# Next-chunk query and key/value products placed among a tile's scores in the index stage of a seven-stage macaron block

## What is computed

```
qi = hadamard((x @ wq_idx).reshape(B, S, Hi, Di))
ki = hadamard(x @ wk_idx)
iw = x @ w_iw
logits = jax.nn.relu(jnp.einsum('bthd,bsd->bhts', qi, ki))
I = jnp.einsum('bth,bhts->bts', iw, logits)
I = jnp.where(causal, I, NEG)
vals, idx = jax.lax.top_k(I, TOPK)
```

## Time and profile before

| | us |
|---|---|
| median of three runs | 2803.31 |
| lowest and highest | 2797.86, 2806.11 |
| profiled execution | 2802.95 |
| its span | 2801.2 |
| index scores and searches, about 1468 to 2030 | 562 |

### The profile page before, as it was taken

The page is one execution under the profiler, slowest core; times in us unless marked ns, Lnnn a source line. Parts: engine busy times, 40 slices in busy tenths (PEclk is TensorE's granted clock), DMA queues, the critical chain, the costliest instruction groups (busy, mean ns, idle before and its releaser), DMA issues. The chain is left out here.

```text
span 2801.2 us, 44746 instructions
## 1 busy us (share of the span) xinstructions
PE 2432.0 (87%) x15815; PEld 1884.3 (67%) x15815; DVE 1718.2 (61%) x3579; ACT 1343.7 (48%) x2718; POOL 1086.9 (39%) x989
## 2 busy tenths in 40 slices
PE   4967899999998986969979898898879998888798
PEld 4855555555555545858867776777668877776687
DVE  7556765756847727554456988979825454545443
ACT  3434355455464453432239868767644443433222
POOL 2542112102112112632317645636356666757232
PEclk9987999999999986989989999999989999999999
DMA  5242000000000003240010000000033233323200
GB/s 164 80 125 73 9 24 9 19 17 19 9 9 19 2 26 120 87 146 31 1 46 1 1 8 1 1 8 9 1 134 89 84 95 89 101 82 100 83 1 30
DMA packets 77332, 136.58 MB, mean 49 GB/s; under 512 B 25792, under 2 KB 47256, under 8 KB 75968
## 3 DMA queue, kind: packets, MB, share of 16 engines
q0 software_dynamic: 26336, 73.01, 8.7%
q1 hardware_dynamic: 50784, 60.72, 6.7%
HBM read 112.48 MB, written 20.81 MB: 48 GB/s over the span
## 5 line engine op out<-in xcount | busy, mean ns | idle before, releaser
L1448 ACT ACTIVATE PT<-ps 128x512 f32<-128x512 f32 (+3 forms) x640 | 298.1, 536 | 336.0 <-PE ps L1205 335.7
L2310 POOL DMA_INDIRECT KV<-kv_scratch,sidx x384 | 368.0, 958 | 213.1 <-issue 131.8
L35 PE MATMUL ps<-KIh,qih 128*128 128x512 f32 (+2 forms) x640 | 247.4, 387 | 50.4 <-DVE Isc L1894 40.0
L1325 DVE TENSOR_REDUCE xn<-ps 128x1 f32<-128x512 f32 x384 | 240.9, 682 | 41.0 <-PE ps L1190 38.7
L1954 POOL TENSOR_TENSOR part_sum<-part_sum,rlp 128x1024 f32<-128x1024 f32 (+7 forms) x120 | 210.6, 1755 | 84.6 <-ACT rlp L1780 83.4
L1894 DVE SCALAR_TENSOR_TENSOR Isc<-ps,iw,Isc 128x1024 f32<-128x1024 f32 (+7 forms) x216 | 208.6, 966 | 50.3 <-ACT ps L1804 45.1
L36 PE MATMUL ps<-KIl,qih 128*128 128x512 f32 (+2 forms) x640 | 239.2, 374 | 0.0
L37 PE MATMUL ps<-KIh,qil 128*128 128x512 f32 (+2 forms) x640 | 238.6, 373 | 0.0
L2232 ACT ACTIVATE sP<-sP,snm 128x128 f32<-128x128 f32 (+2 forms) x256 | 110.4, 432 | 232.8 <-DVE snm L2295 226.7
L1804 ACT ACTIVATE ps<-ps,iwa 128x1024 f32<-128x1024 f32 (+7 forms) x240 | 198.2, 858 | 46.4 <-PE ps L37 45.9
L35 PEld LDWEIGHTS ps<-KIh,qih 128*128 128x128 f32 x640 | 124.2, 194 | 95.0 <-issue 74.0
(11 more groups left out here) (356 smaller groups left out, 6743.6 us busy)
## 6 DMA issues: line engine op xcount, KB each, us to landing
cs<-in_rope SPq DMA_DIRECT2D x20, 512.0 KB, 4.1
ycomb<-y_rows SPq DMA_DIRECT2D x16, 512.0 KB, 4.9
w1raw<-in_w SPq DMA_DIRECT2D x14, 512.0 KB, 6.7
KV<-kv_scratch,sidx POOLq DMA_INDIRECT x384
xn_rows<-xnr SPq DMA_DIRECT2D x8, 512.0 KB, 4.9
w2raw<-in_w SPq DMA_DIRECT2D x14, 256.0 KB, 7.1
wir<-in_wi SPq DMA_DIRECT2D x1, 2176.0 KB, 7.9
X<-in_x SPq DMA_DIRECT2D x1, 2048.0 KB, 8.1
```

The lines of the kernel that those rows point to most:

```text
L35: pe.matmul(out, lhs[0], rhs[0], start=start, stop=False)
L1325: v.tensor_reduce(part, o, AX_X, ALU.max).then_inc(a_free, 1)
L1448: s.activation(PT[:, rnd % 2, hh, lo:CH], ps[:, BANK[kind, u, j, r, hh % 2], lo:CH], ACT.Exp, scale=SCALE).then_inc(a_exp, 1)
L2310: g.indirect_dma_start(KV[:, BG * (k % RB) + m, :], None, a["kv_scratch"], bass.IndirectOffsetOnAxis(sidx[:, t % 2, at:at + 1], 0)).then_i ...
```

## The change

The last pass of tiles 12, 8 and 4 takes in the next chunk's items: behind each of its first four units stands a kv item, and behind each odd head the query pair of that head and the one before it. Only the first chunk is still prepared ahead of its scores. For tiles 12, 8 and 4 the order of the passes is reversed, so that the last one is the 1024-wide one (tile 4 has one pass of 640). The cast of a query pair waits for that pass's unit of the odd head instead of the tile's last unit. `signs` comes after the last subtraction of a chunk, not ahead of the first. The search steps are spread over the units and query pairs of the tile that they now stand in. Nothing is computed that was not before.

```diff
         def iunits(t):
-            return [(h, lo, min(WIDE, (t + 1) * P - lo)) for lo in range(0, (t + 1) * P, WIDE) for h in range(NHI)]
+            starts = list(range(0, (t + 1) * P, WIDE))
+            if t % CT == 0:
+                starts.reverse()
+            return [(h, lo, min(WIDE, (t + 1) * P - lo)) for lo in starts for h in range(NHI)]
+
+        def last_pass(t):
+            return iunits(t)[-1][1]
+
+        def prepared_for(c):
+
+            kv = [("kv", t, 0) for t in reversed(range(CT * c, CT * (c + 1)))]
+            return kv, [("q", NCH - 1 - c, pair) for pair in range(QP)]
+
+        def line(t):
+
+            out, units = [], [(t, h, lo) for h, lo, w in iunits(t)]
+            if t == TILES - 1:
+                kv, q = prepared_for(NCH - 1)
+                out += kv + q
+            if t % CT != 0 or t == 0:
+                return out + units
+            kv, q = prepared_for(t // CT - 1)
+            out += units[:-NHI]
+            for h, unit in enumerate(units[-NHI:]):
+                out.append(unit)
+                if h < CT:
+                    out.append(kv[h])
+                if h % 2 == 1:
+                    out.append(q[h // 2])
+            return out
...
         for t_ in TILE_ORDER:
...
+            for key_ in line(t_):
+                QUEUE[key_] = inumber
+                inumber += 1
+                if key_[0] == t_:
+                    SCORED[key_] = iscored
+                    PASSED[t_, key_[2]] = ipassed // NHI
+                    iscored, ipassed = iscored + 1, ipassed + 1
...
-            return POOLED * (PASSED[t, (passes(t) - 1) * WIDE] + 1)
+            return POOLED * (PASSED[t, last_pass(t)] + 1)
...
+            for key in ITEMS:
+                room(key)
+                o = ibanks(key)
+                if key[0] == "kv":
...
+                elif key[0] == "q":
...
+                else:
+                    t, h, lo = key
+                    d, w = NCH - 1 - t // CT, min(WIDE, (t + 1) * P - lo)
+                    tok = slice(t % CT * P, (t % CT + 1) * P)
+                    pe.wait_ge(i_ql, QP * d + h // 2 + 1)
...
                     s.wait_ge(i_q, QP * d + pair + 1)
-                    if d >= 1 and pair == 0:
-                        s.wait_ge(i_L, SCORED[CT * (c + 1), NHI - 1, (passes(CT * (c + 1)) - 1) * WIDE] + 1)
+                    if d >= 1:
+                        t = CT * (NCH - d)
+                        s.wait_ge(i_L, SCORED[t, 2 * pair + 1, last_pass(t)] + 1)
...
-                s.wait_ge(i_iw, 4 * (d + 1))
...
+                    s.wait_ge(i_iw, 4 * (NCH - t // CT))
+                    s.wait_ge(i_L, SCORED[key] + 1)
...
+            for t in TILE_ORDER:
+                p = TILES - 1 - t
+                todo = [key for key in line(t) if key[0] != "kv"]
+                first = [key for key in todo if key[0] == t][0]
+                steps_done = 0
+                for at, key in enumerate(todo):
+                    if key[0] == "q":
+                        d, pair = key[1:]
+                        v.wait_ge(i_qh, QP * d + pair + 1)
+                        v.tensor_tensor(qil[:, 2 * pair:2 * pair + 2, :].rearrange("p h t -> p (h t)"), ibanks(key),
+                                        qih[:, 2 * pair:2 * pair + 2, :].rearrange("p h t -> p (h t)").bitcast(F32),
+                                        ALU.subtract).then_inc(i_ql, 1)
+                        if pair == QP - 1:
                             signs(d)
...
+                    while p >= 1 and steps_done < (at + 1) * searches(t + 1) // len(todo):
+                        topk_step(t + 1, steps_done)
+                        steps_done += 1
```

More of the change, by code:

```diff
@@ L1712, in room @@
                         pe.wait_ge(i_A, added(*before))
[L1714 to L1719, removed]
+            for key in ITEMS:
+                room(key)
+                o = ibanks(key)
+                if key[0] == "kv":
+                    tok = slice(key[1] * P, (key[1] + 1) * P)
                     for k in range(KD):
-                        i = product(pe, ibanks(key)[:, 0:KVI], (XTh[:, k, tok], XTl[:, k, tok]),
+                        i = product(pe, o[:, 0:KVI], (XTh[:, k, tok], XTl[:, k, tok]),
                                     (ikv_h[:, k, :], ikv_l[:, k, :]), k == 0, k == KD - 1)
                     i.then_inc(i_kv, 1)
[L1724 to L1727, removed]
+                elif key[0] == "q":
+                    d, pair = key[1:]
                     for m in range(2):
@@ L1730, in index_tensor @@
                         for k in range(KD):
-                            i = product(pe, o[:, CH * m:CH * (m + 1)], (wih[:, h, k, :], wil[:, h, k, :]), xt(k, c), k == 0, k == KD - 1)
+                            i = product(pe, o[:, CH * m:CH * (m + 1)], (wih[:, h, k, :], wil[:, h, k, :]), xt(k, NCH - 1 - d),
+                                        k == 0, k == KD - 1)
                     i.then_inc(i_q, 1)
[L1733 to L1744, removed]
+                else:
[3 more added lines that the diff above has]
+                    pe.wait_ge(i_ql, QP * d + h // 2 + 1)
+                    for at in range(0, w, CH):
+                        wide = max(min(CH, w - at), 2 * P)
+                        i = product(pe, o[:, at:at + wide], (qih[:, h, tok], qil[:, h, tok]),
+                                    (KIh[:, lo + at:lo + at + wide], KIl[:, lo + at:lo + at + wide]), True, True)
+                    i.then_inc(i_L, 1)
             pe.wait_ge(i_k, SEARCHED[-1] + 1)
@@ L1780, in signed @@
                 s.activation(at, at, ACT.Copy, scale=iws[:, t, h:h + 1]).then_inc(i_sg, 1)
-            for d in range(NCH):
-                c = NCH - 1 - d
-                for t in reversed(range(CT * c, CT * (c + 1))):
+            for key in ITEMS:
+                if key[0] == "kv":
+                    t = key[1]
                     p = TILES - 1 - t
-                    o = ibanks(("kv", t, 0))
+                    o = ibanks(key)
                     s.wait_ge(i_kv, p + 1)
@@ L1791, in index_scalar @@
                     s.copy(kvs[:, p % 2, :], o[:, 0:2 * P]).then_inc(i_kve, 1)
-                for pair in range(QP):
+                elif key[0] == "q":
+                    d, pair = key[1:]
                     s.wait_ge(i_q, QP * d + pair + 1)
-                    if d >= 1 and pair == 0:
-                        s.wait_ge(i_L, SCORED[CT * (c + 1), NHI - 1, (passes(CT * (c + 1)) - 1) * WIDE] + 1)
-                    s.copy(qih[:, 2 * pair:2 * pair + 2, :].rearrange("p h t -> p (h t)"), ibanks(("q", d, pair))).then_inc(i_qh, 1)
@@ new lines, in index_scalar @@
+                    s.copy(qih[:, 2 * pair:2 * pair + 2, :].rearrange("p h t -> p (h t)"), ibanks(key)).then_inc(i_qh, 1)
+                else:
+                    t, h, lo = key
+                    w = min(WIDE, (t + 1) * P - lo)
+                    o = ibanks(key)[:, 0:w]
+                    s.wait_ge(i_iw, 4 * (NCH - t // CT))
+                    s.wait_ge(i_L, SCORED[key] + 1)
+                    if h in VH:
+                        s.activation(o, o, ACT.Relu, scale=iwa[:, t, h:h + 1]).then_inc(i_R, 1)
+                        if before:
+                            signed(*before)
+                        before = None
+                    else:
+                        if before:
+                            signed(*before)
+                        m = counted(t, h, lo)
+                        if m >= RL:
+                            s.wait_ge(i_B, summed(*PKEYS[m - RL]))
+                        s.activation(rlp[:, m % RL, 0:w], o, ACT.Relu, scale=iwa[:, t, h:h + 1]).then_inc(i_R, 1)
+                        before = (t, h, lo, w) if h in SH else None
@@ L1903, in scores @@
                     i.then_inc(i_A, 1)
[L1905 to L1912, removed]
-                            signs(d)
[L1914 to L1925, removed]
@@ new lines, in index_vector @@
+            for t in TILE_ORDER:
[5 more added lines that the diff above has]
+                    if key[0] == "q":
+                        d, pair = key[1:]
+                        v.wait_ge(i_qh, QP * d + pair + 1)
[3 more added lines that the diff above has]
+                        if pair == QP - 1:
+                            signs(d)
+                    else:
+                        h, lo = key[1:]
+                        if p >= 2 and key == first:
+                            v.wait_ge(i_k, SEARCHED[t + 1])
+                        scores(t, h, lo, min(WIDE, (t + 1) * P - lo))
+                    while p >= 1 and steps_done < (at + 1) * searches(t + 1) // len(todo):
+                        topk_step(t + 1, steps_done)
+                        steps_done += 1
```

## The result

| | before | after |
|---|---|---|
| median of seven runs each, us | 2803.31 | 2816.37 |
| lowest and highest | 2797.86, 2811.17 | 2813.73, 2823.95 |
| profiled execution, its span | 2802.95, 2801.2 | 2813.73, 2811.9 |
| first score product to the first of tile 0 | 546.30 | 556.46 |

The ratio on record is 1.0040, 95% interval 1.0026 to 1.0054; the medians are 13 us apart. The changed kernel is slower by a little more than the 0.3% that can be told from no change, and its median lies outside the range of 2795 to 2811. The forecast of 2804.4 is 12 us too low.

What follows compares the result with a forecast made beforehand. TensorE was taken to bound chunk preparation and the wide pass right after it, VectorE the later passes. The terms −10.0 + 2.95 + 7.1 + 1.5 gave +1.5 us on 2802.95, so 2804.4 us, range 2795 to 2811.

Steps and rivals of the forecast that it cites:

- step 3: Hosts (passes of tiles 12, 8, 4 taking in the next chunk's items) end earlier on TensorE: 10.0 us gained.
- step 4: Behind the hosts, signs at the last pair start ACT 1.8 us later; 7.05 of the 10.0 us is left.
- Step 6: At the start, chunk 0 in tile 15 has the later signs and no gain: 1.5 us lost.
- Step 5: Behind the hosts, search steps pushed out of the query stretch lengthen the windows: 7.1 us given back.
- Step 1: TensorE's work in a host: 47.23 us for tiles 12 and 8, 41.63 for tile 4.
- Step 2: Reversed passes of tiles 12 and 8 cost nothing: their narrow passes stay at 19.50 and 10.65 us.
- Not all will lie at one end together: On the sum of all bounds, 2796.0 to 2814.8 us: the terms won't all reach their good or bad ends.
- the ring stalls in the host: Rival: slots free too late in the hosts, 0.5 us in each of 24 groups, 2816 us; chance 0.14.
- TensorE decides to the end: Rival: tiles behind hosts are paced by TensorE and ACT, no steps given back, 2793 us; chance 0.16.
- the clock: Rival: a low-clock stretch falls inside a host, 3.4 us each, two 6.8, 2808 to 2811 us; chance 0.08.

Runs made afterwards that it cites:

- kernel 1: Changed kernel with the signs after the second query pair instead of the last: scores stretch 549.29 us, ratio to before 1.0023.
- kernel 10: The changed kernel run and profiled again, nothing altered: 2818.23 us, ratio to before 1.0054, scores stretch 556.60 us.
- kernel 5: Changed kernel with the kv items behind the first four query pairs and signs at the fifth pair: scores stretch 542.79 us, ratio to before 0.9987.
- kernel 11: Same code as kernel 5, run on the first kind of chip: 2802.56 us, ratio to before 0.9991, scores stretch 546.52 us.
- kernel 8: Kernel 1 with all four kv items ahead of the host's first unit: scores stretch 549.24 us, ratio to before 1.0004.
- kernel 4: Changed kernel without the reversed passes of tiles 12 and 8: scores stretch 556.60 us, ratio to before 1.0057.
- kernel 3: Kernel before with no search steps beside the query pairs of chunks 1 to 3: scores stretch 551.41 us, ratio to before 1.0022.
- kernel 9: Kernel before with kv items behind query pairs 0 to 3 and signs at the fifth pair: 2804.40 us, ratio 0.9998, scores stretch 544.07 us.
- kernel 2: Kernel before with only the signs moved after the last subtraction: scores stretch 551.86 us, ratio to before 1.0014.

## Why the prediction was wrong

The forecast's mechanism held: what TensorE gained in the hosts was given back behind them. Its sizes did not: the gain (step 3) was 3.8 us, not 10.0, and the signs (steps 4 and 6) cost 5.2 to 7.2, not 4.45. The three terms, read on TensorE from the first score product of the host tile to the next chunk's first, and behind that:

| step | forecast, us | measured | by what |
|---|---|---|---|
| 3, hosts end earlier | −10.0 | −3.8 | windows before and after |
| 4 and 6, signs | +2.95 and +1.5 | +7.2, of which 5.2 in the tiles where they act | kernel 1; kernel 10 |
| 5, search steps | +7.1 | +6.6 | kernel 1 against before |
| sum | +1.5 | +10.0 | +10.2 in the stretch |

The terms are differences of single profiles, good to a microsecond or two each; in kernel 10 the hosts end 2.3 us earlier in sum, with a low clock in tile 12's narrow pass.

**Step 1** was right. Kernels 5 and 11 show wide hosts of 47.32 to 47.43 us for the 47.23 worked out. A full-width score unit still takes 1.40 us for its six products, 0.2333 each. The Trainium skill (TensorE: Matmul & The Clock Gate, "Wait — 56ns, not 53.3ns?") gives 215.7 ns; these products don't reach that.

**Step 3** is the one that failed most. "The same slots are waited for in the new order; I keep these": the pauses were 8.6 us, not 4.34, and thus at the upper bound in sum (twice). The reason, as far as kernels 5 and 8 show it, is that the queue behind the slot had changed. Before, kv items and long pairs filled the ring while VectorE had nothing else to do; in the new order each second slot holds a score unit that is added by VectorE, and the items between are the shortest of all, 0.77 us. Kernels 5 and 8 tell this apart: the same items in another order give 2.0, the kv items moved ahead of the entry 7.3. In addition the narrow passes that now come first are longer, from last add to last add 20.1 and 12.0 us against 19.50 and 10.65. So of step 3's 10.0 some 4.3 went into pauses and 2 into those two passes. Step 2 had these at "well under a microsecond", and that was wrong for tile 8, though kernel 4 shows that the reversal as a whole costs nothing.

**Steps 4 and 6** were right in kind and too small by 2.7 us, or by 0.8 if only the four tiles are counted in which the signs act. The wait on ACT was taken as 1.8 us longer than before; the idle time of its first activation rose by 3.05, 2.5 and 2.1 in tiles 11, 7 and 3, and by 1.7 in tile 15. Part is the first sign operation, 1.49 us for 0.18 in tile 11 and 1.04 in tile 7. Part of the 7.2 is the clock: behind the pause of 2.43 us on TensorE it was 0.51 for 3.4 us in one profile, which cost 1.25, and 1.00 in the other, so the pause doesn't decide it by itself. Step 6 alone erred the other way: tile 15 took 45.45 us for 45.06, so the start cost 0.4 and not 1.5.

**Step 5** was right, +7.1 against +6.6 (5.3 in kernel 5, 5.1 in kernel 3). All eleven steps among the units leave VectorE no idle time to fill, as tile 6 had said.

"Not all will lie at one end together" was the wrong way to narrow the range. As I read it, the entry pauses and the signs have one cause in common, VectorE late with the operation that lets another engine go; the pauses came out at their upper bound, and the signs of step 4 had no bound at all. The bad end of the sum, 2814.8, is near the measured time partly by luck: it takes 12.8 us for the steps, which cost 4 to 7. Of the rivals, *the ring stalls in the host* named the right chain (subtraction, step, add) but priced it at 0.5 us in each of 24 groups; there is none in the steady groups (5.55 us each in tiles 12 and 8, 4.84 in tile 4), and 4.3 us more at the three entries. That its 2816 is the measured time is chance. *TensorE decides to the end* was wrong, *the clock* never fell inside a host (granted 1.00 in all three) and mattered behind one.

What stays open: the median differs by 13.1 us and the stage by 10.2. The 4.4 us behind the stage are not explained. They come again: from tile 0's first product to the end it is 787.2 and 786.6 us in the kernel before and kernel 9, and 791.5, 790.9 and 791.6 in the changed kernel, kernel 10 and kernel 11. Ahead of the stage the same three are shorter (1463.9, 1467.1 and 1464.1 against 1467.8 and 1469.7), and the two parts together are 2255 to 2258 in all five, so no loss outside the stage is shown.

## What to carry to other kernels

Moving work of the bounding engine in among other work of the same engine saves only what the other engine did beside it, so ask what that stretch had been hiding (here the search steps and the signs) before counting a gain. Where a ring of buffers is drained by an engine in arrears, give each slot that comes free the longest item: here that order took the pauses from 8.6 to 2.0 us, and with no interleave it shortened the preparations of the kernel before by 3.7, though neither made the whole measurably faster than before. Small operations that another engine waits for belong well ahead of their reader.

## What the runs showed of the hardware

A small VectorE operation ran on until a GpSimd operation beside it ended. GpSimd's add at the end of a pass, at the two places where the first sign operation was slow:

```profile
1676.93 2.40 POOL L1982 TENSOR_TENSOR Isc<-Isc,part_sum 128x1024 f32<-128x1024 f32 x1 [6.31 <-DVE Isc L1916]
...
1862.42 2.41 POOL L1982 TENSOR_TENSOR Isc<-Isc,part_sum 128x1024 f32<-128x1024 f32 x1 [5.78 <-DVE Isc L1916]
```

By its rows it ends at 1679.33 and 1864.83, the sign operation at 1679.39 and 1864.88. Kernel 1 has it at another operation of the signs, 1.44 us, and another GpSimd line:

```profile
1971.80 1.44 DVE L1879 TENSOR_SCALAR iw<-iw 128x64 f32<-128x64 f32 x1
```

```profile
1971.62 1.58 POOL L1977 TENSOR_TENSOR part_sum<-part_sum,rlp 128x640 f32<-128x640 f32 x1 [11.00 <-ACT rlp L1800]
```

Those end at 1973.24 and 1973.20. In kernel 2 no GpSimd operation runs beside any of the sixteen sign operations, and they take 0.18 to 0.23 us, as its expectation said they would if GpSimd is the cause. The Trainium skill (SBUF — State Buffer, "Who interferes with whom") says that VectorE and GpSimd share a pair of ports that one holds exclusively; by that rule a sign operation waits out the add. The coincidence of the ends agrees in each of these cases. Kernel 2 has another order besides, and no kernel took away GpSimd's add alone, so that the ports are the cause isn't shown by an experiment.

Further, a low clock falls in different places from one execution of a kernel to the next: kernels 5 and 11 are the same code with hosts equal to 0.02 us, and their stretches differ by 3.7. The changed kernel paused for 2.43 us at the same unit in both of its profiles, and the granted clock behind it was 0.51 in one and 1.00 in the other.
